# A graph attention layer on one core: M's scale from column maxima, G(0) ahead of hg(0), edge types checked by GpSimd and PE, second round reordered

## What is computed

```python
h = relu(layernorm(x))
dep_emb = dep_emb_table[adj]
hi = h @ W1_w[:384] (per i) + dep_emb @ W1_w[384:] + W1_b
hj = h @ W2_w[:384] (per j) + dep_emb @ W2_w[384:] + W2_b
relevance[i, j] = sum(hi * hj)
A = softmax(where(adj != 0, relevance, -1e9))
out = x + relu((A @ h) @ gcn_w + gcn_b) @ Wo_w + Wo_b
```

## Time and profile before

| | us |
|---|---|
| median of 3 runs | 378.17 |
| lowest, highest | 377.02, 379.87 |
| profiled execution | 379.19 |
| its span, first to last instruction | 377.3 |
| PE busy | 358.4 (95%) |
| DVE, ACT, GpSimd busy | 268.2, 273.7, 178.3 |
| before the loop's steady part, to 76.5 | 76.5, of which PE busy 62.29 |
| steady part, 76.5 to 364.5 | 288.0, all of it PE busy |

### The profile page before, as it was taken

How to read it: one execution, slowest core, us unless ns; L and a number is a source line. 1 busy time by engine, 2 the same in 40 slices (tenths; PEclk the granted TensorE clock), 3 DMA queues, 4 the chain that set the end, 5 groups by cost and what they waited for, 6 DMA issues and landing times.

```text
span 377.3 us, 9541 instructions
## 1 busy us (share of the span) xinstructions
PE 358.4 (95%) x3154; PEld 222.8 (59%) x3154; DVE 268.2 (71%) x665; ACT 273.7 (73%) x580; POOL 178.3 (47%) x349
## 2 busy tenths in 40 slices
PE   7899883999999999999999999999999999999986
PEld 6564542656575656656565757566665656575653
DVE  1688878659686877777694958677776859576674
ACT  2375679297969788787879697887878787964733
POOL 2017506647372728274655637282836565490000
PEclk9889998799999999999999999999999999999999
DMA  8972412439564839384654646393937543434043
GB/s 237 287 246 80 108 65 50 119 104 171 151 164 130 203 83 250 84 220 114 187 126 133 156 140 175 97 236 83 250 83 199 135 127 78 132 87 147 19 123 130
DMA packets 82215, 53.87 MB, mean 143 GB/s; under 512 B 45666, under 2 KB 82148, under 8 KB 82196
## 3 DMA queue, kind: packets, MB, share of 16 engines
q1 hardware_dynamic: 81492, 52.64, 51.7%
q10 hardware_dynamic: 640, 0.79, 0.7%
q0 software_dynamic: 64, 0.20, 0.3%
HBM read 17.44 MB, written 12.58 MB: 80 GB/s over the span
## 4 chain that ended last, share of the span: by engine, by line
PE 87%; DVE 5%; ACT 4%; DMA 2%; issue 1%; ACTq 0%; DVEq 0%
PE bank L1028 23%; PE bank L1029 23%; PE bank L1030 23%; PE bank L1106 6%; PE bank L1260 3%; PE bank L1255 3%; PE bank L1080 2%; DMA e_col<-L_gnn_dep_emb_table_dram 2%; PE bank L1222 1%; ACT bank L611 1%; ACT h_parts L451 1%; ACT h_tok L460 1%; PE bank L1323 1%; ACT h_tok L451 1%; PE bank L1325 1%
## 5 line engine op out<-in xcount | busy, mean ns | idle before, releaser
L402 POOL TENSOR_TENSOR h_parts<-h_tok,h_parts 128x1536 f16<-128x1536 f32 x14 | 43.4, 3098 | 99.0 <-ACT h_parts L451 99.0
L1028 PE MATMUL bank<-gw_hi,hT 128*128 128x385 f16 (+2 forms) x204 | 65.2, 324 | 7.6 <-DVE hg_lo L712 6.1
L1030 PE MATMUL bank<-gw_hi,hT 128*128 128x385 f16 (+2 forms) x204 | 64.9, 323 | 0.0
L1029 PE MATMUL bank<-gw_lo,hT 128*128 128x385 f16 (+2 forms) x204 | 64.8, 322 | 0.0
L1028 PE MATMUL bank<-wo_hi,z_hi 128*128 128x384 f16 x180 | 58.7, 326 | 0.0
L1029 PE MATMUL bank<-wo_lo,z_hi 128*128 128x384 f16 x180 | 58.7, 326 | 0.0
L1030 PE MATMUL bank<-wo_hi,z_lo 128*128 128x384 f16 x180 | 58.7, 326 | 0.0
L408 POOL TENSOR_TENSOR x_all<-x_all,bo_all 128x1536 f32 (+1 forms) x16 | 56.2, 3520 | 0.0
L1028 PE MATMUL bank<-hT,m_hi 128*128 128x512 f16 x144 | 54.6, 379 | 0.0
L1030 PE MATMUL bank<-hT,m_lo 128*128 128x512 f16 x144 | 54.6, 379 | 0.0
L1029 PE MATMUL bank<-hT,m_hi 128*128 128x512 f16 x144 | 54.6, 379 | 0.0
(11 more groups left out here) (149 smaller groups left out, 679.7 us busy)
## 6 DMA issues: line engine op xcount, KB each, us to landing
x_all<-in_x_dram SPq DMA_DIRECT2D x16, 768.0 KB, 6.4
out_dram<-x_all SPq DMA_DIRECT2D x15, 768.0 KB, 4.0
hg_parts<-hg_lo SPq DMA_DIRECT2D x32, 192.0 KB, 3.0
hg_parts<-hg_hi SPq DMA_DIRECT2D x32, 192.0 KB, 3.2
out_dram<-x_all SPq DMA_DIRECT2D x4, 192.0 KB, 1.9
x_all<-in_L_gnn_W_w_dram SPq DMA_DIRECT2D x1, 576.0 KB, 5.5
x_all<-in_L_gnn_W_w_dram ACTq DMA_DIRECT2D x1, 576.0 KB, 6.1
gcn_raw<-in_L_gnn_gcn_w_dram SPq DMA_DIRECT2D x1, 576.0 KB, 10.1
```

The source lines that it names most:

```text
L402: nc.gpsimd.tensor_tensor(h_parts[:, :, 1, :], h_tok[:, :, :], h_parts[:, :, 0, :], ALU.subtract).then_inc(h_split, 1)
L1028: nc.tensor.matmul(dst, lh, rh, start=(c == 0), stop=False)
L1029: nc.tensor.matmul(dst, lh, rl, start=False, stop=False)
L1030: last = nc.tensor.matmul(dst, ll, rh, start=False, stop=(c == DC - 1))
```

## The change

1. M's scale comes from a bound: the column maxima of W1 and W2 (w_top) multiplied and summed over partitions by a product with ones on PE. M stays in PSUM; ACT makes m_hi and DVE m_lo straight from the banks. DVE computes first_coefficients behind that scale.
2. ACT copies W2's transpose as well as W1's. The norms of gcn and Wo are made together and go through one pair of transposes and one product.
3. PE does G(0) before hg(0), and hg(0) has the 385th column, so that the separate narrow products for the row terms of supertile 0 go. Wo's high part is made in the first round.
4. Two groups of six filler products (keep_warm) are put on PE.
5. Edge types: GpSimd writes max(adj-1, 0) as f16 in two halves, PE sums them over partitions in eight products with ones16, DVE reduces the row.
6. The loads: W2 from SP, x(1), Wo and adj without a wait for x(0); the small ones from ACT's queue, e_col first. statistics(2) has its own tile.
7. The second round is written out: normalise(2) is spread around attention_out and G(1)'s chunks on ACT; on DVE wo_lo stands behind attention_high, and statistics(3) after G(1,2).

The diff, cut to its core:

```diff
@@ sync @@
             sp.dma_start(w1_raw, W1[0:D, :].rearrange("(c p) e -> p c e", p=P)).then_inc(w1_loaded, 16)
+            sp.dma_start(w2_raw, W2[0:D, :].rearrange("(c p) e -> p c e", p=P)).then_inc(w2_loaded, 16)
             load_x(0)
             sp.dma_start(gcn_raw[:, :, 0:D], gcn_w.rearrange("(c p) e -> p c e", p=P)).then_inc(gcn_loaded, 16)
-            sp.wait_ge(x_loaded, 16)
+            sp.dma_start(wo_raw[:, :, :], Wo.rearrange("(c p) e -> p c e", p=P)).then_inc(wo_loaded, 16)
             load_x(1)
@@ gpsimd @@
+            def types_excess(n):
+
+                pool.wait_ge((adj_loaded, adj_rest_loaded)[n], 16)
+                half = adj_all[:, n * HALF:(n + 1) * HALF, :].rearrange("p t j -> p (t j)")
+                nc.gpsimd.tensor_scalar(excess[n], half, -float(EDGE), 0.0, ALU.add, ALU.max).then_inc(type_excess, 1)
...
+            types_excess(0)
             make_bias(0)
+            types_excess(1)
             main_coefficients(1)
             make_bias(1)
+            main_coefficients(2)
@@ scalar @@
+            for c in range(DC):
+                act.wait_ge(w_transposed, DC + c + 1)
+                nc.scalar.activation(w2T[:, c, 0:D], bank[3 + c][:, 0:D], ACT.Copy).then_inc(w_copied, 1)
             gcn_norm()
-            m_copy(0)
-            m_copy(1)
+            wo_norm()
+            for d in range(DC):
+                m_high_part(d)
             early_normalise(0, range(EARLY_WIDE, KT))
...
+            def second_round():
+                for c in range(DC):
+                    early_high_part(1, c)
+                move_scores(0)
+                g_high_part(1, 0)
+                g_whole(0)
+                exponentials(0)
+                g_high_part(1, 1)
+                g_whole(1)
+                normalise(2, range(0, 1))
+                attention_out(1)
+                normalise(2, range(1, 2))
+                g_high_part(1, 2)
+                g_whole(2)
+                normalise(2, range(2, KT))
+                aggregated(1)
+                move_scores(1)
+                normalise(3, range(0, 2))
+                exponentials(1)
+                normalise(3, range(2, KT))
@@ vector @@
+            dve.wait_ge(w_copied, DC)
+            nc.vector.tensor_reduce(w_top[:, 0, :], w1T, AX.X, ALU.max, apply_absolute_value=True).then_inc(top_step, 1)
...
+            nc.vector.tensor_tensor(w_bound[:, :], w_top[:, 0, :], w_top[:, 1, :], ALU.mult).then_inc(bound_ready, 1)
 
             statistics(0)
+            dve.wait_ge(bound_wide, 1)
+            nc.vector.tensor_scalar(peak[:, SC_M:SC_M + 1], bank[7][:, BOUND], TINY, None, ALU.max).then_inc(scale_step, 1)
+            scales(SC_M, SC_M + 1, 1)
...
             first_coefficients()
...
+            for c in range(DC):
+                g_low_part(0, c)
+            dve.wait_ge(pair_bias_made, 2)
+            for k in range(DC):
+                rows_and_low(0, k)
             statistics(2)
+            rows_and_low(0, DC)
+            dve.wait_ge(type_row, 1)
+            nc.vector.tensor_reduce(type_top[:, :], bank[7][0:1, :], AX.X, ALU.max).then_inc(type_step, 1)
...
+            def second_round():
                 for c in range(DC):
                     early_low_part(1, c)
+                dve.wait_ge(bias_made, 1)
+                masked_scores(0)
+                g_low_part(1, 0)
+                attention(0, prev=False)
+                g_low_part(1, 1)
+                attention_high(1, prev2=False)
+                dve.wait_ge(wo_high, 1)
+                low_part(wo_lo[:, :, :], wo_raw[:, :, :], wo_hi[:, :, :], SC_WO).then_inc(wo_split, 1)
+                g_low_part(1, 2)
+                statistics(3)
                 dve.wait_ge(bias_made, 2)
+                aggregated(1)
@@ tensor @@
+            def gcn_ready(d):
+                pe.wait_ge(gw_split, d + 1)
+                if d == 0:
+                    pe.wait_ge(gw_vector, 1)
...
+            for c in range(DC):
+                g_chunk(c, 0, chunk_ready(0) if c == 0 else None)
+                if c == 0:
+                    pe.wait_ge(norms_top, 1)
+                    nc.tensor.matmul(bank[6][:, NORM_WIDE], ones[0:1, :], norm_top[0:1, :], start=True,
+                                     stop=True).then_inc(norms_wide, 1)
             for k in range(KT):
+                if k == DC:
+
+                    pe.wait_ge(g_split, 1)
+                hg_tile(0, k, 0, gcn_ready if k == 0 else None)
+
+            pe.wait_ge(consts_made, 1)
+            pe.wait_ge(pairs_copied, DC + 2)
+            PIECES = HALF * S // 512
+            for n in range(2):
+                pe.wait_ge(type_excess, n + 1)
...
```

More of the change, by code:

```diff
@@ L549, in _ @@
                                  scale=scale[:, SC_M:SC_M + 1]).then_inc(gw_high, 1)
-            for c in range(DC):
-                if c == DC - 1:
-                    early_normalise(1, range(KT))
+            for c in range(1, DC):
                 g_high_part(0, c)
                 g_whole(c)
+            hg_high_part(0, 0)
+            act.wait_ge(wo_scale_ready, 1)
+            nc.scalar.activation(wo_hi[:, :, :], wo_raw[:, :, :], ACT.Copy,
+                                 scale=scale[:, SC_WO:SC_WO + 1]).then_inc(wo_high, 1)
@@ L556, in _ @@
+            for k in range(1, KT):
+                hg_high_part(0, k)
+            early_normalise(1, range(KT))
             with typed(act):
@@ L563, in _ @@
                 act.wait_ge(ty_free, NSUP + 1)
-            for c in range(DC):
-                early_high_part(1, c)
             def attention_out(s):
@@ L603, in iteration, with exponentials @@
                                          ACT.Copy).then_inc(score_copied, 1)
-                if nxt2 and prev:
-                    normalise(s + 2, range(0, 2))
-                if not prev:
-                    g_high_part(1, 0)
-                    g_whole(0)
+            def exponentials(s):
                 act.wait_ge(exp_bias_ready, s + 1)
@@ L1048, in _ @@
                     last.then_inc(w_transposed, 1)
[L1050 to L1058 removed]
+                if n == 0:
+                    keep_warm(KEEP_WARM, 7)
             pe.wait_ge(dep_loaded, 16 * 4)
@@ new lines, in _ @@
+            pe.wait_ge(consts_made, 1)
+            pe.wait_ge(pairs_copied, DC + 2)
+            PIECES = HALF * S // 512
+            for n in range(2):
+                pe.wait_ge(type_excess, n + 1)
+                for piece in range(PIECES):
+                    last = nc.tensor.matmul(bank[7][0:1, :], ones16[:, :], excess[n][:, piece * 512:(piece + 1) * 512],
+                                            start=(n == 0 and piece == 0), stop=(n == 1 and piece == PIECES - 1))
+            last.then_inc(type_row, 1)
@@ new lines, in transposed_attention @@
+            def transposed_attention(s):
+                pe.wait_ge(att_ready, s)
+                if not isinstance(s, int) or s >= 2:
+                    pe.wait_ge(attT_high, GT * (s - 1))
+                    pe.wait_ge(attT_copied, s - 1)
+                else:
+                    pe.wait_ge(ident16_made, 1)
+                for k in range(KT):
+                    last = nc.tensor.transpose(attT_bank[:, k, :, :], att_parts[:, k, :, :], ident16[:, :])
+                last.then_inc(attT_done, 1)
@@ L1304, in iteration, with output @@
+            def output(s):
                 pe.wait_ge(z_split, DC * s)
```

550 lines of the change are left out of this document (232 added, 318 removed).

## The result

The changed kernel takes 396.68 us (median of 4 runs, 395.63 to 397.01) against 377.70 for the kernel before in the same session (4 runs, 377.02 to 379.87): 1.0483 times as long, with a 95% interval of 1.0446 to 1.0519. The prediction was 382.7 with a range of 375 to 386. The direction was right, the size was not.

What follows compares the result with a forecast made beforehand. PE bounds the kernel, busy from 76.5 to 364.5 us; only the start up to T(2) can move. +2.1 there, +1.6 and +0.8 for clock drops at T(2) and T(1) make +4.5: 378.17 becomes 382.7 us, range 375 to 386.

Steps and rivals of the forecast that it cites:

- start to T(0): From the start to PE's first transposes of h: 28.15 us, against 20.24 before the change.
- T(0) to T(1): From PE's first transposes of h, through G(0) and hg(0), past the types branch: T(1) at 47.9 us, +6.5.
- T(1) to token_low(2): From PE past the types branch to GpSimd's token_low(2), when normalise(2) ends on ACT: 16.1 us, a gain of 2.45.
- token_low(2) to T(2): From GpSimd's token_low(2) to PE's attention transposes in the second loop round: 18.5 us, T(2) at 82.5 against 80.40.
- T(2) to the end of the span: Pure PE work behind the second round's attention transposes, where a clock drop is paid in full: 1.6 us added.
- The collision: Ahead of T(0), GpSimd's three 1.90 us instructions and DVE's coefficient steps exclude each other: +4.0 us, bounds 0 and 5.5.
- rival (c): Warm-ups don't keep the clock up in M's product: M 1.6 us later, mostly hidden; +5, 383.2; 0.55 with the forecast.
- Rival (a): Ahead of T(0), DVE's coefficients pass before or beside GpSimd's instructions: the 4.0 goes, sum +0.5, 378.7 us; chance 0.22.
- the chain behind normalise(2): GpSimd, ACT and DVE work from token_low(2) to att_parts, 19.58 us before the change; PE can't pass T(2) before it.
- the clock drop of 12.6 to 15.7: PE's half clock during M's product, taken as gone with PE kept busy: products at 0.65 us each, six until 16.35.
- rival (d): Clock drops hit G(0) too, as PE stands from 24.15 to 28.15: +6, 384 us; chance 0.08.
- The drop at T(2): Lower PE clock after a 3.4 us stall at the second round's attention transposes: 1.6 us, bounds 0 and 2.4.

Runs made afterwards that it cites:

- e2: The changed kernel with GpSimd's type check as add and mult in place of add and max; 387.11 us, ratio 1.0211.
- g1: The changed kernel with the type check as Relu on ACT and GpSimd's bias behind its coefficients of supertile 1; 383.90 us, ratio 1.0163.
- e7: e2 with GpSimd's add_bias(0) moved behind the coefficients of supertile 3 in round 1; 383.23 us, ratio 1.0125.
- g2: e2 without both keep-warm groups on PE; 387.17 us, ratio 1.0243.
- e5: e2 with DVE's first coefficients ahead of the bound, all four h_tok(0) tiles on ACT, no keep-warm group ahead of T(0); 381.68 us, ratio 1.0099.
- f2: f1 with the type check as two Relu on ACT, GpSimd making only the bias, behind its coefficients of supertile 1; 377.59 us, ratio 0.9983.
- f1: e5 and e7 together, the type check still a product over signed sums; 377.20 us, ratio 0.9970.

## Why the prediction failed, step by step

The error is 14.0 us (396.68 less 382.7). By the marks, measured distance against the predicted one:

| step | predicted | measured | error |
|---|---|---|---|
| start to T(0) | 28.15 | 37.13 | +9.0 |
| T(0) to T(1) | 19.75 | 22.30 | +2.55 |
| T(1) to token_low(2) | 16.1, and 0.8 for the clock | 17.51 | +0.6 |
| token_low(2) to T(2) | 18.5 | 18.70 | +0.2 |
| T(2) to the end of the span | 296.9, and 1.6 for the clock | 299.46 | +1.0 |
| median less profiled span | 0.9 | 1.58 | +0.7 |

**The collision was the right mechanism at a wrong size.** The step that failed is the duration of GpSimd's instructions: of types_excess(0), make_bias(0) and types_excess(1) the prediction says that "each reads 128x2048 from SBUF, 1.90 us". The 1.90 was taken from make_bias, an add and a mult, and given to an add and a max. Each check measured 7.10, and the two held DVE's coefficients until 35.67 where 26.8 was put. This term alone is 9.6 us of the error of 14.0 (e2 against the changed kernel). I had bounded the loss at 5.5 us from above "if all of the three instructions (5.7 us) add up"; that bound was no bound, since it rested on the same unshown duration. Where the trace before doesn't show an operation, its duration wanted a range of its own. With the duration at 1.90 (e2), T(0) came at 28.53, so the rest of the sum to T(0) held to 0.4.

That closeness is in part luck. In e2 the bound was at 18.7 instead of 17.15 (rival (c), and hidden behind GpSimd as it said), and the steps are 17, not the 15 that the working counts. They took 7.4 us (19.65 to 27.07) for 8.65 and ended 0.3 behind the 26.8, since the end of GpSimd's third instruction, 25.0, sets their end. "Whole instructions at a time" held beside the short ones only: beside a 7.10 us check the two-input steps came free 2.6 us before its end.

**Rival (a), no collision, was priced too low.** I gave it 378.7; g1 measures it at 383.9. T(0) was 2.1 later than its 24.15 (the bound 2.0 late), T(0) to T(1) took 20.4 for 19.75 with the two Relu on ACT, which the rival doesn't have, and T(1) to token_low(2) 17.8 for 16.1: the gain there, put at 2.45, is 0.8 to 1.1 in g1, e2 and the changed kernel. e2 shows the same, as it takes the check's length out: of the 4.4 us by which it lies above the forecast, 0.4 are T(0), 1.4 T(0) to T(1), 0.6 T(1) to token_low(2) beyond the 0.8 for the clock, 0.15 from there to T(2), 1.0 behind T(2), and 0.9 the median against its profile (387.11 less 385.3 for 0.9).

**T(2) hangs on the chain behind normalise(2): right**, shown by e7. The wait there was put at 3.4 us, "over 2 us" as a sign, and measured 1.85 (1.77 in e2). token_low(2) to T(2), predicted 18.5, took 18.65 to 18.85 wherever the changed kernel's order of GpSimd stood. wo_lo at 1.42 and gw_lo at 0.23, PE's stall before the last hg tile at 2.54 ("about 2.6"), adj's landing at 19.1 ("I take 19.0"), and the branch at 1.57 ("1.43") were right.

**The clock.** "I take the clock drop of 12.6 to 15.7 as gone" was wrong: 0.50 at 13 us after too. In g2 it is there without the keep-warm groups as in e2 with them. The drop behind the long wait ahead of T(0) is rival (d), which I gave 0.08: the clock was 0.51 from 37 to 43 us, and T(0) took 2.82 us for 1.53. T(0) and G(0)'s first chunk together took 6.4 us (37.13 to 43.55) for 3.95, and 4.5 in g1, where the clock was back at 1.00 by 28 us: this is most of the 2.55 from T(0) to T(1). The drop at T(2), taken as 1.6 us, cost 2.6 in the changed kernel (299.46 for 296.9).

**What the case doesn't settle.** How much of e5's gain is the removal of its keep-warm group alone, and what the bound in place of M's maxima is worth by itself, weren't tried.

## What to carry to other kernels

Price an instruction by engine and operation, not by its shape: a row with the same tile and another ALU operation is no row for it, and its duration gets a range of its own. Before work is given to GpSimd, list what DVE runs in that window, since a 0.15 us step waited up to 4.35 us beside a 7 us instruction and an h_tok tile 7.33, and moving the step away hands the wait to the next in DVE's queue. Another engine may do the work at no cost that can be told (here ACT, 1.99 us; f2 against f1). And follow the chain into the first instruction at which the bottleneck engine waits: reordering two neighbours there was worth 3.9 us, and nothing in the kernel where the wait was 0.3 us.
